# A mixture-of-experts stage that fetches its rows by a slot table and adds its results into the output by indirect DMA

## The reference, cut to what matters

```python
x = x + ga * attn(layernorm(x) * (1 + ca) + sa)      # (4, 1024, 256)
h = layernorm(x) * (1 + cb) + sb
# experts, for each token of h (4096 tokens, 256 wide)
logits = h @ router_w.T                              # 8 experts
topk_logits, topk_idx = top_k(logits, 2)
probs = softmax(topk_logits)
hmid = gelu(h @ w1[e].T + b1[e])                     # 512 wide
y_e = hmid @ w2[e].T + b2[e]
x = x + gb * sum(probs_e * y_e over the two experts)
```

## Time and profile before

| | us |
|---|---|
| median of 3 runs (lowest, highest) | 2835.69 (2832.26, 2842.91) |
| the profiled execution | 2830.93 |
| its span, first to last instruction | 2829.3 |

### The profile page before, as it was taken

One profiled execution on the slowest core, in us unless ns is written; L12 is line 12 of the kernel. 1 busy time (PEld: TensorE's weight loads), 2 busy tenths in 40 slices (PEclk: granted clock), 3 DMA queues, 4 the chain that ended last, 5 costly groups with the idle time before them and its releaser, 6 DMA issues. The chain is left out here.

```text
span 2829.3 us, 103823 instructions
## 1 busy us (share of the span) xinstructions
PE 2121.2 (75%) x47244; PEld 1451.7 (51%) x47244; DVE 1502.9 (53%) x2594; ACT 784.8 (28%) x1302; POOL 959.1 (34%) x1333
## 2 busy tenths in 40 slices
PE   3568887877887877878887787864777726999970
PEld 2235545545555555556555455553677713666640
DVE  5165665656666666665665666645877421222225
ACT  0242332333433433423433323311222011111111
POOL 0055246244254354354353452402433052000016
PEclk7698898999899999997998998966988657999985
DMA  2000101000011010010010010016321322111124
GB/s 84 22 2 18 28 18 30 19 27 28 18 29 28 19 29 26 20 29 26 16 29 22 18 29 22 18 32 258 109 69 51 122 78 69 53 49 53 49 66 147
DMA packets 83689, 131.69 MB, mean 47 GB/s; under 512 B 13297, under 2 KB 57473, under 8 KB 82065
## 3 DMA queue, kind: packets, MB, share of 16 engines
q1 hardware_dynamic: 77106, 108.22, 11.9%
q0 software_dynamic: 6144, 16.79, 1.9%
HBM read 76.45 MB, written 48.50 MB: 44 GB/s over the span
## 5 line engine op out<-in xcount | busy, mean ns | idle before, releaser
L679 DVE SCALAR_TENSOR_TENSOR d_S<-d_S,gamma_chunk,d_ps 128x64 f32<-128x64 f32 x960 | 226.7, 279 | 429.0 <-PE d_ps L1038 426.8
L872 PE MATMUL d_ps<-hT,d_w 128*128 128x512 f32 x768 | 416.6, 642 | 18.2 <-DVE d_qk L656 11.9
L516 ACT ACTIVATE d_U<-d_ps 128x128 f32<-128x128 f32 x512 | 141.3, 276 | 853.4 <-PE d_ps L1029 852.8
L1038 PE MATMUL d_ps<-d_U,d_ktok 64*32 64x128 f32 x3968 | 232.9, 302 | 75.5 <-ACT d_U L516 68.7
L607 POOL TENSOR_TENSOR d_tmp<-d_Tq,d_TT 128x31 f32<-128x31 f32 (+15 forms) x496 | 249.1, 502 | 111.9 <-DVE d_TT L751 74.3
L612 POOL TENSOR_TENSOR d_TT<-d_TT,d_tmp 128x31 f32<-128x31 f32 (+15 forms) x496 | 266.4, 537 | 38.9
L1029 PE MATMUL d_ps<-d_S,d_WT 64*32 64x64 f32 x3968 | 165.4, 238 | 117.7 <-DVE d_S L679 110.5
L656 DVE SCALAR_TENSOR_TENSOR d_qk<-d_ps,d_cw,d_qk 128x1023 f32<-128x1023 f32 (+2 forms) x192 | 242.9, 1279 | 17.7 <-ACT d_qk L480 14.8
L1029 PEld LDWEIGHTS d_ps<-d_S,d_WT 64*32 64x32 f32 x3968 | 82.5, 109 | 303.5 <-DVE d_S L679 245.9
L1038 PEld LDWEIGHTS d_ps<-d_U,d_ktok 64*32 64x32 f32 x3968 | 91.1, 113 | 221.9 <-ACT d_U L516 144.7
L1806 POOL DMA_INDIRECT hT<-made_scratch,m_pos_i x64 | 61.9, 967 | 400.0 <-DMA made_scratch<-hT 380.9
(11 more groups left out here) (213 smaller groups left out, 4086.5 us busy)
## 6 DMA issues: line engine op xcount, KB each, us to landing
y_scratch<-d_yT SPq DMA_DIRECT2D x256, 64.0 KB, 1.8
d_arow<-ab_scratch SPq DMA_DIRECT2D x128, 128.0 KB, 3.0
y<-y_scratch SPq DMA_DIRECT2D x8, 2048.0 KB, 8.6
rows_scratch<-o_zero SPq DMA_DIRECT2D x1, 9088.0 KB, 40.5
hT<-rows_scratch SPq DMA_DIRECT2D x71, 128.0 KB, 2.2
made_scratch<-hT SPq DMA_DIRECT2D x71, 128.0 KB, 1.7
m_w<-w_in SPq DMA_DIRECT2D x16, 512.0 KB, 10.2
xs<-x_in SPq DMA_DIRECT2D x4, 1024.0 KB, 7.9
```

Source lines behind the costliest of these rows:

```text
L516: nc.scalar.activation(U[:, c % KEPT].rearrange("p b v -> p (b v)"), u_ps(c), ACT.Identity).then_inc(s_ue, 1)
L679: last = nc.vector.scalar_tensor_tensor(out=S[:, (c + 1) % SLOTS, b2, :], in0=S[:, c % SLOTS, b2, :], scalar=gC[:, b2, tc * NCH + c:tc * N ...
L872: return nc.tensor.matmul(dst[:, g, :], w[:, m % 2, n, dc, :], hT[:, dc, at:at + G], start=(dc == 0), stop=(dc == DC - 1))
L1038: last = nc.tensor.matmul(ps[quad(h, kh), 1, 0:2 * DH], ktok[rows64(h), tc % 2, c, here(kh)], U[rows64(h), c % KEPT].rearrange("p b v -> p ...
```

## The change

- In `attn_out`: `x1` is no longer held whole, but in a ring of four groups; each group is loaded, completed and stored to `out` in DRAM, which becomes a plain table of 4096 + 128 rows. The high part of the split is made by ACT, the low part by DVE. Four gate buffers instead of two, two PSUM buffers for the product instead of four. The router logits are made here per group, and the normalised rows are turned back, copied by ACT and stored to a table in DRAM (`h2_d`, 512 columns wide: left half the row, right half the gate row `gb` of its batch, written once per batch by a broadcast). 9 MB of zeros are no longer written.
- In the head of `moe`: no scatter. DVE makes for each of the 64 x 128 pairs a one-hot row over 71 tiles and one over 128 rows; 64 products on PE, accumulated, give a table [slot, tile] of token number and of weight. Empty slots point behind the 4096 rows. The first bias is made for every tile at once by a small product.
- In the loop: POOL fetches the rows of tile i by one indirect DMA with its column of the slot table (512 columns a row, ring of 4). No bias products. The hidden rows are copied by DVE as they come from the up product, turned, and then activated by ACT in four pieces with the bias as its per-partition operand. DVE adds the second bias (its expert's number in a register of DVE), multiplies by the slot's weight and the gate row that was fetched, and POOL adds the tile into `out` by an indirect DMA with add, each after the one before has landed. Fetch i waits for the eviction of tile i-4.
- The end of `moe` is gone.

The diff, cut to its core and moved left by 8 columns:

```diff
+XRING = 4
+YRING = 4
...
-po = st.enter_context(nc.psum_tensor("o_po", [P, 4, G], F32))
+po = st.enter_context(nc.psum_tensor("o_po", [P, 2, G], F32))
+pb = st.enter_context(nc.psum_tensor("o_pb", [P, 2, D], F32))
...
-    sp.dma_start(x1[:], x).then_inc(s_l, 16)
...
+    for g in range(XRING):
+        load_x(g)
...
+    for b in range(B):
+        sp.dma_start(h2_d[b * T:(b + 1) * T, D:].rearrange("(j p) d -> p j d", p=P),
+                     gates[:, 1, b, :].rearrange("p (a d) -> p a d", a=1).broadcast_to([P, NT, D])).then_inc(s_ho, 16)
+    for k in range(NG + 2):
+        if k + 2 < NG:
+            sp.wait_ge(s_ys, M * (k + 1))
+            load_y(k + 2)
+        if k and k - 1 + XRING < NG:
+            sp.wait_ge(s_n, k)
+            sp.wait_ge(s_xo, 16 * (k + 1))
+            load_x(k - 1 + XRING)
+        if k < NG:
+            sp.wait_ge(s_x1, GT * (k + 1))
+            sp.dma_start(tiles(out, k, D), held(k)).then_inc(s_xo, 16)
+        if k >= 2:
+            sp.wait_ge(s_rw, 2 * (k - 1))
+            sp.wait_ge(s_ho, 16 * (1 + B + k - 2))
+            sp.dma_start(tiles(h2_d, k - 2, D), rows[:, k % 2]).then_inc(s_ho, 16)
+    sp.wait_ge(s_ho, 16 * (1 + B + NG))
+    sp.wait_ge(s_xo, 16 * (1 + NG))
...
+        for m in range(M):
+            if 1 <= g <= NG:
+                i = (g - 1) * M + m
+                if m == 0 and g >= 2:
+                    act.wait_ge(s_op, GT * (g - 1))
+                act.wait_ge(s_m, i + 1)
+                nc.scalar.activation(y_sp[:, 0, m, :].bitcast(F32R), y[:, (g - 1) % 2, m, :],
+                                     ACT.Identity).then_inc(s_yh, 1)
+            if g < NG:
                 i = g * M + m
                 act.wait_ge(s_gp, i + 1)
-                if i >= 2:
-                    act.wait_ge(s_m, i - 1)
-                nc.scalar.activation(g_sb[:, i % 2, :], pg[:, i % 2, :], ACT.Silu,
+                if i >= 4:
+                    act.wait_ge(s_m, i - 3)
+                nc.scalar.activation(g_sb[:, i % 4, :], pg[:, i % 2, :], ACT.Silu,
                                      bias=bg_sb[:, m:m + 1]).then_inc(s_g, 1)
+        if g >= 3:
+            for k in range(2):
+                act.wait_ge(s_bk, 2 * (g - 3) + k + 1)
+                if k == 0 and g >= 5:
+                    act.wait_ge(s_ho, 16 * (1 + B + g - 4))
+                nc.scalar.activation(rows[:, (g - 3) % 2, 2 * k:2 * k + 2, :], pb[:], ACT.Identity).then_inc(s_rw, 1)
...
-            dve.wait_ge(s_m, g * M + m + 1)
-            split([y_sp[:, a, m, :] for a in range(2)], y[:, g % 2, m, :], s_ys)
+            dve.wait_ge(s_yh, g * M + m + 1)
+            low(nc, y_sp[:, 1, m, :], y[:, g % 2, m, :], y_sp[:, 0, m, :]).then_inc(s_ys, 1)
...
-            if i >= 4:
-                pe.wait_ge(s_t, i - 3)
+            if i >= 2:
+                pe.wait_ge(s_t, i - 1)
...
+    def logits(g):
+        pe.wait_ge(s_e, g + 1)
+        for j in range(g * GT, (g + 1) * GT):
+            for dc in range(DC):
+                nc.tensor.matmul(pl[:, j * E:(j + 1) * E], h2T[:, dc, j * P:(j + 1) * P], rw_sb[:, dc, :],
+                                 start=(dc == 0), stop=(dc == DC - 1))
+
+    def rows_back(g, k):
+        if 2 * g + k:
+            pe.wait_ge(s_rw, 2 * g + k)
+        for j in range(2):
+            for dc in range(DC):
+                at = g * G + (2 * k + j) * P
+                last = nc.tensor.transpose(pb[:, j, dc * P:(dc + 1) * P], h2T[:, dc, at:at + P], ident[:])
+        last.then_inc(s_bk, 1)
+
     pe.wait_ge(s_ws, 2)
-    for g in range(NG + 2):
+    for g in range(NG + 3):
         if g < NG:
             gate(g)
+        if g >= 3:
+            logits(g - 3)
+            rows_back(g - 3, 0)
         if 1 <= g <= NG:
             product(g - 1)
-        if g >= 2:
+        if g >= 3:
+            rows_back(g - 3, 1)
+        if 2 <= g < NG + 2:
             turned(g - 2)
...
+        act.wait_ge(s_tab, 2)
+        nc.scalar.activation(b1_t[:].rearrange("p f s -> p (f s)"), b1_p, ACT.Identity).then_inc(s_x, 1)
+        act.wait_ge(s_x, 2)
+        for j in range(SLOT_TILES):
+            act.wait_ge(s_th, j + 1)
+            if j >= 2:
+                act.wait_ge(s_dn, j - 1)
+            for f in range(FC):
+                last = nc.scalar.activation(hm[:, j % 2, f * P:(f + 1) * P], ps[:, 2, f * P:(f + 1) * P], ACT.Gelu,
+                                            bias=b1_t[:, f, j:j + 1])
+            last.then_inc(s_ge, 1)
...
-        pool.wait_ge(s_pos, 1)
-        pool.wait_ge(zeroed, 16)
-        for i in range(NTOK):
-            pool.wait_ge(s_rk, i + 1)
-            for a in range(2):
-                nc.gpsimd.indirect_dma_start(rows_s, bass.IndirectOffsetOnAxis(ap=pos_i[:, a, i:i + 1], axis=0),
-                                             rows[:, i % RROWS, :], None).then_inc(s_sc[i % RROWS], 16)
-        for k in range(RINGS):
-            pool.wait_ge(s_st[k], 16 * len(range(k, SLOT_TILES, RINGS)))
-        for i in range(NTOK):
-            if i >= 4:
-                pool.wait_ge(s_o, i - 3)
-            for a in range(2):
-                nc.gpsimd.indirect_dma_start(yg[:, i % 4, a, :], None, made_s,
-                                             bass.IndirectOffsetOnAxis(ap=pos_i[:, a, i:i + 1], axis=0)
-                                             ).then_inc(s_sc[i % RROWS], 16)
+        for c in range(K // KC):
+            pool.wait_ge(s_r, 2 * c + 1)
+            nc.gpsimd.tensor_tensor(hot[:, part(c), 0, :], tile_hot[:, part(c), :], wide(tokens(c), SLOT_TILES),
+                                    ALU.mult).then_inc(s_tk, 1)
+        pool.wait_ge(s_id, 1)
+        for i in range(SLOT_TILES + XRING):
+            if i >= XRING:
+                pool.wait_ge(s_ev, i - XRING + 1)
+            if i < SLOT_TILES:
+                nc.gpsimd.indirect_dma_start(xt[:, i % XRING, :], None, h2_d,
+                                             bass.IndirectOffsetOnAxis(ap=slot_i[:, i:i + 1], axis=0)
+                                             ).then_inc(s_ga[i % XRING], 16)
+            if i >= XRING:
+                j = i - XRING
+                if j:
+                    pool.wait_ge(s_sct, 16 * j)
+                nc.gpsimd.indirect_dma_start(out, bass.IndirectOffsetOnAxis(ap=slot_i[:, j:j + 1], axis=0),
+                                             yo[:, j % YRING, :], None, compute_op=ALU.add).then_inc(s_sct, 16)
+        pool.wait_ge(s_sct, 16 * SLOT_TILES)
...
+        flat_w = wts.rearrange("p a n -> p (a n)")
+        for c in range(K // KC):
+            nc.vector.tensor_tensor(tile_hot[:, part(c), :], mwide(iota, KC), wide(tile_of[:, part(c)], SLOT_TILES),
+                                    ALU.is_equal).then_inc(s_r, 1)
+            nc.vector.tensor_tensor(row_hot[:, part(c), :], mwide(iota_row, KC), wide(row_of[:, part(c)], P),
+                                    ALU.is_equal)
+            dve.wait_ge(s_r, 2 * c + 1)
+            nc.vector.tensor_tensor(hot[:, part(c), 1, :], tile_hot[:, part(c), :], wide(flat_w[:, part(c)], SLOT_TILES),
+                                    ALU.mult).then_inc(s_r, 1)
...
+        dve.wait_ge(s_tab, 1)
+        step(nc.vector.tensor_scalar(empty, table[:, 0:SLOT_TILES], 0.0, pidx, ALU.is_equal, ALU.mult))
+        step(nc.vector.scalar_tensor_tensor(out=slot_f, in0=table[:, 0:SLOT_TILES], scalar=float(NONE), in1=empty,
+                                            op0=ALU.add, op1=ALU.add))
+        nc.vector.tensor_copy(slot_i[:], slot_f).then_inc(s_id, 1)
...
+        for i in range(-1, SLOT_TILES + 2):
...
-            if i >= 1:
-                j = i - 1
-                dve.wait_ge(s_th, j + 1)
-                if j >= 2:
-                    dve.wait_ge(s_dn, j - 1)
-                nc.vector.tensor_copy(hm_s[:, j % 2, :], ps[:, 2 + j % 2, :]).then_inc(s_hs, 1)
-        for i in range(NTOK):
-            dve.wait_ge(s_rk, NTOK + i + 1)
-            u = yg[:, i % 4, 1, :]
-            nc.vector.scalar_tensor_tensor(out=u, in0=u, scalar=wts[:, 2, i:i + 1], in1=yg[:, i % 4, 0, :],
-                                           op0=ALU.mult, op1=ALU.add).then_inc(s_hi, 1)
-            dve.wait_ge(s_hi, 2 * i + 1)
-            nc.vector.tensor_tensor(u, u, gates[:, 1, i // NT, :], ALU.mult).then_inc(s_hi, 1)
-            dve.wait_ge(s_hi, 2 * i + 2)
-            nc.vector.tensor_tensor(x1[:, i, :], x1[:, i, :], u, ALU.add).then_inc(s_o, 1)
-        dve.wait_ge(s_o, NTOK)
+                nc.vector.tensor_copy(xs[:, j % 2, :], ps[:, 5 + j % 2, 0:D]).then_inc(s_xs, 1)
+            if 0 <= i < SLOT_TILES:
+                dve.wait_ge(s_up, i + 1)
+                if i >= 2:
+                    dve.wait_ge(s_th, i - 1)
+                nc.vector.tensor_copy(raw[:, i % 2, :], ps[:, i % 2, :]).then_inc(s_uk, 1)
+            if i >= 2:
+                j = i - 2
+                e = nc.vector.value_load(eid_i[0:1, j:j + 1], min_val=0, max_val=E - 1)
+                dve.wait_ge(s_dn, j + 1)
```

(24 more changed lines are left out.)

318 lines of the change are left out of this document (134 added, 184 removed).

## The result

| | before, us | after, us |
|---|---|---|
| median (lowest, highest) of 4 runs each | 2836.19 (2832.26, 2842.91) | 3146.65 (3138.01, 3151.50) |
| ratio after to before, 95% interval | | 1.1089 (1.1055 to 1.1122) |
| the profiled execution, its span | 2830.93, 2829.3 | 3148.84, 3147.3 |
| mean granted clock of PE | 0.862 | 0.839 |

The change makes the kernel 11% slower: 310 us by the medians, 318 by the spans of the two profiled executions. First the stages, as windows (start:end, length, busy time and count of PE, PEld, DVE, ACT, POOL, then clock, DMA share, GB/s): projection, head, loop, end. They answer to the earlier trace rows.

A forecast was written before the change was run, and what follows sets the result against it. PE was taken to bound the old loop, POOL's indirect DMAs its head and end. Loop +454, head -82, end -84, projection -36 sum to +252 on 2830.9, so 3083; predicted 3085 us, range 2890 to 3215.

The forecast's parts named there:

- bare wait: Expert loop: after each down product PE waits 4.5 us for eviction (0.98), POOL's start (0.28) and fetch (3.28).
- PE's part of a turn: Expert loop: PE's own work, 4.65 us at full clock, takes 7.3 with part of it at half rate.
- loop: Expert loop: 67 turns of 11.8 us plus 35 make 826 us against 372, +454.
- head: Start of the expert stage: logits, row scatters and first load go, one-hot products come; about 49 us, -82.
- end: End of the expert stage: 90.9 us go, one last eviction and adding scatter remain, 7 us; -84.
- projection: Output projection: PE becomes the bound, a turn falls from 34.2 to 27 us; -36 in total (-65 to -5).
- register load on DVE: Expert loop: between DVE's copy and its wait for down; taken at nothing, 1 us a turn as the bad end.
- The clock: Expert loop: idle PE drops to half rate for 5 to 5.8 us of each turn's work; mean clock 0.7 to 0.85.
- the clock stays up: Rival, expert loop: full clock despite the waits, turns of 9.15 us, kernel at 2900 us; 12%.
- the adding scatter sets the turn: Rival, expert loop: landing above about 10 us delays POOL's next fetch; a landing of 12 gives about 3200 us; 6%.
- the ring does not bind: Rival, expert loop: no wait for a free place, 71 turns of 4.49 us, kernel about 2575; 8% shared with the other faster case.
- rival with a turn of 7.0: Rival, expert loop: wait only 2.3 us in all, kernel about 2745 us; 8% shared with the other faster case.

The follow-up runs named there:

- experiment 6: Changed kernel with four places, the fetch bringing 1 KB of each row instead of 2 (gate row left out): 3051.3 us, a turn of 11.09 against 12.18.
- experiment 9: Kernel before the change, without its two bias products in a turn of the expert loop: 2774.7 us, a turn of 4.10.
- experiment 4: Changed kernel with four places, PE kept busy by 32 useless transposes after each down product: 2995.7 us, a turn of 10.07.
- experiment 3: Changed kernel with four places, only PE's register load moved ahead of the wait for the fetched rows: 3052.6 us, a turn of 11.07.
- experiment 1: Changed kernel with eight places instead of four for fetched rows, some semaphores merged and a buffer shared: 2591.5 us, ratio to before 0.9096.
- experiment 5: Changed kernel with five places instead of four, some semaphores merged and a buffer shared: 2639.8 us, a turn of 5.03.
- Experiment 10: Changed kernel with eight places, POOL's multiplications in projection and head moved to DVE: 2562.1 us, ratio to before 0.901.
- experiment 7: Changed kernel with eight places, its scatters without the addition: 2592.0 us, against 2591.5 with it.

## Why the prediction was right, and where it was off

I predicted 3085 us (2890 to 3215); it is 3146.7. The mechanism was right in place and cause: PE waits behind each down product, 67 times, for eviction and fetch, and the clock falls with it. The price of the wait was right by its parts, that of PE's part of a turn partly by luck. By the steps:

| step | predicted | measured |
|---|---|---|
| bare wait in a turn | 4.5 us | 4.75 |
| PE's part of a turn | 7.3 (without a load) | 7.5 (1.15 before the up product in it) |
| turn | 11.8 | 12.23 |
| loop | +454 | +468 |
| head | -82 (49 long) | -76.5 (54.9) |
| end | -84 (7 long) | -75.3 (15.6) |
| projection | -36 (-65 to -5) | -16.5 |
| sum | +252 | +300, and 18 ahead of what was changed |

**The bare wait** was built from the earlier trace rows, and each piece held: eviction with DVE's start 1.09 us (0.98 predicted), POOL 0.28 (0.28), fetch 3.39 (3.28). The 0.48 for the second KB is 0.54 by experiment 6. By the Trainium skill's page "DMA: Bandwidth & Descriptors", section "Anatomy of one DMA — SWDGE (gpsimd) path", the fetch was estimated to land in 2.6 us; it was 3.4.

**PE's part** came out near by errors that cancel, which is luck: 0.4 too much of products, 0.9 too little for a load, and some 0.4 too much for the clock. The removed bias products were sized by their own distances, 0.73, and cost 1.13 (experiment 9), so PE's turn alone is 4.10 and not 4.49. The register load was given up to 0.42 and taken at nothing; the gap that it opens is 0.93 at full clock in every turn (experiment 4), and moving it gains 1.1 with what the clock gives back (experiment 3). No run takes the load away at full clock behind such a wait, so a part of the 0.93 may be PE's restart; of the gap at low clock 0.65 goes with the load. The register load on DVE, also taken at nothing, does not show: DVE starts 0.15 us after the down product. The rows of before could not show PE's, and I looked for it behind the wrong cover: not the bias product hid it but PE's full queue. In experiments 1 and 9 there is no bias product and yet no such gap in a turn without a wait; it appears where PE has drained in a wait just before, even a short one (experiment 5).

**The clock** was taken at 2.65 us a turn (7.3 less 4.65), from 5 to 5.8 us at half rate. It is about 2 (experiment 4), and the low level is not equally long in all turns: under 5 us in the turn shown, at least 5.9 in the next (0.50 from 2613.1 to 2619.0). The Trainium skill's "TensorE: Matmul & The Clock Gate", section "HAM oscillation — how this bites in real kernels", was right on this: the trace has 0.75 in the loop, and 0.98 when PE is kept busy with useless products.

**The end** was sized for one scatter; one was under way and two were to be issued, and the last issue came 7.1 us after PE's end where the sum had 1.3. The step that counts what is queued failed: the last tiles wait for no fetch, and come quicker than the scatters follow each other (4.5 us apart). The rest of the miss, 3 us, lies behind the last issue: 8.5 us to the span's end where the sum had 4 to 6, and there no run shows why.

**Head and projection** failed in one and the same step: DVE's operations were priced from rows where POOL did nothing. Beside POOL's products they take 3.22 for 1.34, and 1.65 (11.6 in seven) for 0.69; the second pair stood in the trace of before already. Experiment 10 removes this and gives the 27 us turn back; its projection is 39.8 us shorter than that of before, where the sum had 36, and its head takes the 49.9 us for which the sum had 49. The Trainium skill's page "SBUF — State Buffer", section "Who interferes with whom", says that a DVE instruction with two SBUF inputs contends with a GpSimd instruction that reads SBUF, and that the order of issue decides which of the two is held up. The traces agree: L1920 (2.28), issued 0.16 before POOL's product, runs at its usual speed and POOL's takes 4.06; L1923, issued under it, is the one held up. Had I weighed that rule, with the 1.67 us of before beside it, the projection's turn would have come out nearer to 30 than to 27.

**The rivals.** That the clock stays up (2900) is what experiment 4 makes by force: 2996; it was priced too low, by the load (0.93 in 67 turns, 62 us) and by the shortfall of head, end and projection (34 us). That the adding scatter sets the turn fell: it lands in 3.8 us. The case in which the ring does not bind was priced at 2575, and experiment 1 measures it at 2591.5; that this is so near is luck in part, as the turn was 0.39 shorter than priced (28 us) and the other parts gained less. The rival with a turn of 7.0 has a slip: by its own terms it gives 2759 and not 2745, and nothing hangs on it. The 2591.5 are the fair value of the change's idea; the four places cost 540 us of it (3131 to 2592).

## What to carry to other kernels

When a buffer gets a second use at the far end of a pipeline, count how many steps it is now held and compare with the ring's length: here one place more gave 490 us, and moving one step behind the work that needs nothing new gave 340. Count too what is still queued when the last product ends. Wait in a queue last, behind all that could go first; a wait on PE costs its own length, here some 40% again in clock (about 2 us for a wait of 4.8), and it bares whatever the full queue had hidden (here a register load of 0.9 us). Price an operation from a row in which its neighbour engine does what it will do beside it.

## What the runs showed of the hardware

- The granted clock of PE is 0.75 in a loop whose turns of 12.2 us have 4.75 us of idle PE, 0.98 when 32 transposes fill most of that wait, and 0.95 with waits of 2.6 us in turns of 7.2.
- A register load on PE between two products costs nothing while PE's queue is full (0.21 us from row transposes to up product); right after a wait that drained it the same distance is 1.15 us at full clock.
- Two small products of 16 rows between PE's products, 0.31 and 0.42 us by their own distances, cost 1.13 together: the neighbours take some 0.1 us longer at each of four borders.
- DVE with two SBUF inputs beside POOL's products: 0.69 becomes 1.65 us, 1.34 becomes 3.22. POOL's 64 gate products (102 us there), given to DVE, took 44 us of DVE and gave 49 back.
- An adding indirect scatter of 128 rows of 1 KB: issue 1.55 to 1.59 us on POOL and landing 3.8, a plain one 0.97 and 2.6 (experiment 7). In a chain one follows another by 4.5 and by 3.2 us.
- An indirect fetch of 128 rows lands in 2.8 us with 1 KB a row and in 3.4 with 2 KB.
